# A two-layer decoder: the wide heads' output product in f16 parts, and one PSUM ring for two kinds of sums

## The reference, cut to what matters

```python
q = (x @ w_q);  k = (cond @ w_k);  v = (cond @ w_v)       # 16 heads of 64
a = softmax(q @ k.T / sqrt(64))                            # 112 x 375 to a head
x = layernorm(x + (a @ v).reshape(b, 112, 1024) @ w_out + b_out)
```

## Time and profile before

| | |
|---|---|
| median of three runs | 1141.89 us (1140.78 to 1142.65) |
| the profiled execution | 1142.11 us, of which the span of its instructions is 1140.3 us |
| TensorE, matmul | 977.3 us busy, 86% of the span |
| TensorE, weight loads | 703.0 us, 62%, beside the matmuls |
| VectorE | 661.8 us, 58% |
| ScalarE | 589.5 us, 52% |
| GpSimd | 285.3 us, 25% |
| granted clock of TensorE, mean | 0.924 of full speed |
| the chain that ended last | TensorE 52%, VectorE 22%, ScalarE 10%, DMA 5% |

### The profile page before, as it was taken

One profiled execution on the slowest core, in us unless ns is written; L12 is line 12 of the kernel. 1 busy time (PEld: TensorE's weight loads), 2 busy tenths in 40 slices (PEclk: granted clock), 3 DMA queues, 4 the chain that ended last, 5 costly groups with the idle time before them and its releaser, 6 DMA issues.

```text
span 1140.3 us, 22115 instructions
## 1 busy us (share of the span) xinstructions
PE 977.3 (86%) x8864; PEld 703.0 (62%) x8864; DVE 661.8 (58%) x1565; ACT 589.5 (52%) x1379; POOL 285.3 (25%) x297
## 2 busy tenths in 40 slices
PE   7987889897879898999898688888889897699995
PEld 4664556665469775567566556666666665447654
DVE  3256545665848855665666477676676664436103
ACT  5532555552548865555544355545555554465741
POOL 3421422100420007121112122122222205132733
PEclk9997878988989999999999899999899798689998
DMA  9351554300769868532261433221221105000001
GB/s 304 108 95 34 122 107 83 96 12 20 245 201 346 292 234 257 178 107 89 78 199 59 116 109 109 82 74 63 83 84 53 28 1 231 1 1 1 1 1 33
DMA packets 66678, 123.71 MB, mean 108 GB/s; under 512 B 11632, under 2 KB 41968, under 8 KB 62496
## 3 DMA queue, kind: packets, MB, share of 16 engines
q1 hardware_dynamic: 64528, 117.48, 33.8%
q0 software_dynamic: 2048, 4.82, 1.4%
HBM read 86.30 MB, written 35.92 MB: 107 GB/s over the span
## 4 chain that ended last, share of the span: by engine, by line
PE 52%; DVE 22%; ACT 10%; DMA 5%; POOL 4%; issue 4%; SPq 1%; DVEq 0%; POOLq 0%; ACTq 0%
PE psum L405 36%; ACT s_p L2738 3%; DVE s_p L2780 3%; DVE s_max L2769 2%; PE psum L1402 2%; PE psum L2708 2%; PE psum L2697 2%; DMA raw_wd<-in_wd 2%; DVE s_pT L2761 1%; POOL got L2003 1%; PE psum L2227 1%; DMA ctx_raw<-in_ctxT 1%; PE psum L560 1%; PE psum L2876 1%; DVE s_max L679 1%
## 5 line engine op out<-in xcount | busy, mean ns | idle before, releaser
L2738 ACT ACTIVATE s_p<-psum,s_max 112x375 f32<-112x375 f32 x128 | 72.2, 569 | 97.6 <-DVE s_max L2769 97.6
L726 POOL TENSOR_TENSOR rstd<-meanvar,minus_half 112x1 f32<-112x1 f32 x40 | 25.1, 629 | 244.7 <-DVE meanvar L671 174.2
L679 DVE TENSOR_REDUCE s_max<-psum 112x2 f32<-112x750 f32 x64 | 59.4, 934 | 35.7 <-PE psum L560 35.0
L2697 PE MATMUL psum<-ident,s_p 112*125 112x112 f32 x384 | 62.7, 296 | 8.9 <-DVE s_p L2780 4.2
L2769 DVE TENSOR_REDUCE s_max<-psum 112x1 f32<-112x375 f32 x128 | 63.7, 539 | 1.9 <-PE psum L2689 1.9
L2697 PEld LDWEIGHTS psum<-ident,s_p 112*125 112x125 f32 x384 | 51.3, 198 | 19.0 <-DVE s_p L2780 6.1
L3079 POOL TENSOR_TENSOR rs<-ms,minus_half 112x32 f32<-112x32 f32 x8 | 43.5, 5440 | 77.5 <-DVE ms L3013 77.5
L2689 PE MATMUL psum<-s_k,s_q 64*112 64x375 f16 x384 | 46.5, 348 | 18.5 <-ACT s_p L2738 6.3
L405 PE MATMUL psum<-Wv,ctx 128*125 128x512 f16 x240 | 58.6, 394 | 3.5 <-issue 2.7
L405 PE MATMUL psum<-ctx,Wk 128*128 128x375 f16 x320 | 61.5, 327 | 0.0
L3397 POOL TENSOR_TENSOR hidden<-raw,hidden 128x448 f16<-128x448 f32 x44 | 45.5, 1036 | 54.8 <-ACT hidden L3280 53.0
(11 more groups left out here) (381 smaller groups left out, 2465.1 us busy)
## 6 DMA issues: line engine op xcount, KB each, us to landing
keys<-s_k SPq DMA_DIRECT2D x64, 187.5 KB, 2.3
s_k<-keys SPq DMA_DIRECT2D x8, 1500.0 KB, 7.6
values<-s_v SPq DMA_DIRECT2D x48, 224.0 KB
s_v<-values SPq DMA_DIRECT2D x16, 672.0 KB
raw_wg<-in_wg SPq DMA_DIRECT2D x8, 1024.0 KB, 6.7
raw_wu<-in_wu SPq DMA_DIRECT2D x8, 1024.0 KB, 7.0
raw_wd<-in_wd SPq DMA_DIRECT2D x8, 1024.0 KB
s_kd<-k_halves SPq DMA_DIRECT2D x48, 93.8 KB, 3.8
```

What stands on the lines that cost most here:

```text
L679: VE.tensor_reduce(s1_max[b % 2][:, 2 * p:2 * p + 2], rings["s1"][unit][0:N, :, 0:S], X, ALU.max, negate=True).then_inc(*V.up("max1", n))
L2697: ins = TE.transpose(rings["t4"][unit][0:SCH, c * N:(c + 1) * N], p[:, c * SCH:(c + 1) * SCH], ident[0:N, 0:N])
L2738: SC.activation(rings["p4"][2 * n + j], rings["s4"][(n, j)][0:N, 0:S], ACT.Exp, bias=s4_max[b % 2][:, h:h + 1], accum_out=s4_sum[b % 2][:, ...
```

## The change

The output weights of the wide heads are split into f16 parts in stage 3, by ScalarE and VectorE, in a second `w4s` unit placed when the fourth `out` is placed. The raw weights now lie behind the raw query weights; the parts need the memory that the raw weights had. ScalarE's copy `oT4` writes f16, and a new unit `oT4l` has VectorE make the low part from the same bank, behind ScalarE. `s4_heads` places it one turn after `oT4`, ahead of the next group's sums; it, and no longer `oT4`, releases the bank, and `s4_out` waits for it. The output product is 24 f16 products in place of 8 f32 ones, and the add is the scaled one. The banks 6 and 7 become one ring for the wide and the causal sums.

```diff
-    Wq4 = g_w4.load(Region(nc, wts.base + keys_at, 20 * KB), "Wq4", [P, KC, HW])
-    Wq4_16 = ringm.tensor("Wq4_16", [P, 2, KC, HW], F16)
-    Wo4 = g_w4.load(ringm, "Wo4", [P, HW // P, D])
+    raw_w4 = Region(nc, wts.base + keys_at, 20 * KB)
+    w4_raw = {"Wq4": g_w4.load(raw_w4, "Wq4", [P, KC, HW]),
+              "Wo4": g_w4.load(raw_w4, "Wo4", [P, HW // P, D])}
+    w4_16 = {"Wq4": ringm.tensor("Wq4_16", [P, 2, KC, HW], F16),
+             "Wo4": ringm.tensor("Wo4_16", [P, 2, HW // P, D], F16)}
     bout4 = g_w4.load(ringm, "bout4", [N, D])
-    s4_attT = ringm.tensor("s4_attT", [P, HW // P, N])
+    s4_attT = ringm.tensor("s4_attT", [P, 2, HW // P, N], F16)
...
     def s3_ahead():
         yield from until(("out", 3, 2))
-        yield [("w4s",)]
+        yield [("w4s", "Wq4")]
+        yield from until(("out", 3, 3))
+        yield [("w4s", "Wo4")]
         yield from until(("k4put", 0, HP - 1), ("out", 3, 3))
...
             elif what == "w4s":
+                name, = at
                 act.wait_ge(g_w4.ready, V["got", 2, B - 1])
-                SC.activation(Wq4_16[:, 0], Wq4[:], ACT.Copy, scale=WSCALE).then_inc(*A.up("w4s"))
+                SC.activation(w4_16[name][:, 0], w4_raw[name][:], ACT.Copy,
+                              scale=WSCALE).then_inc(*A.up("w4s", name))
...
             elif what == "w4s":
-                dve.wait_ge(A["w4s",])
-                VE.scalar_tensor_tensor(Wq4_16[:, 1], Wq4[:], WSCALE, Wq4_16[:, 0], ALU.mult,
-                                        ALU.subtract).then_inc(*V.up("w4s"))
+                name, = at
+                dve.wait_ge(A["w4s", name])
+                VE.scalar_tensor_tensor(w4_16[name][:, 1], w4_raw[name][:], WSCALE, w4_16[name][:, 0],
+                                        ALU.mult, ALU.subtract).then_inc(*V.up("w4s", name))
...
-    w4 = banks(0, 6, by_release=True)
-    rings.update(s4=w4, t4=w4, misc4=w4, misc5=w4, o4=banks(6, 1), o5=banks(7, 1),
+    w4, sums = banks(0, 6, by_release=True), banks(6, 2, by_release=True)
+    rings.update(s4=w4, t4=w4, misc4=w4, misc5=w4, o4=sums, o5=sums,
                  p4=Ring(s4_p), pT4=Ring(s4_pT), sc5=Ring(sc5), pT5=Ring(pT5))
...
     step("oT4", "A oT4")
+    step("oT4l", "V oT4")
...
                 yield [("sc4", n)]
+            if o > 0 and o % 4 == 0:
+                place(("oT4l", (o - 1) // HP, (o - 1) % HP // 4))
             if 0 <= o < B * HP:
                 if o % 4 == 0:
                     yield from until(("vget", o // 4))
-                    rings["o4"].take(o // 4, (A, ("oT4", o // HP, o % HP // 4)))
+                    rings["o4"].take(("o4", o // 4), (V, ("oT4", o // HP, o % HP // 4)))
                 yield [("av4", o)]
...
     def s4_out(b):
-        yield from until(("oT4", b, 1))
+        yield from until(("oT4l", b, 1))
...
-                    rings["o5"].take(at[0], (A, ("oT5", at[0])))
+                    rings["o5"].take(("o5", at[0]), (A, ("oT5", at[0])))
...
             elif what == "out":
                 s, b = at
-                pe.wait_ge(A["oT4", b, 1], *rings["misc4"].free(unit))
+                pe.wait_ge(V["oT4", b, 1], V["w4s", "Wo4"], *rings["misc4"].free(unit))
                 mm(rings["misc4"][unit][0:N, 0:D],
-                   [(s4_attT[:, k, :], Wo4[:, k, :]) for k in range(HW // P)], T.up("out", 4, b))
+                   [(s4_attT[:, u, k, :], w4_16["Wo4"][:, v, k, :])
+                    for k in range(HW // P) for u, v in PARTS], T.up("out", 4, b))
...
-                SC.activation(s4_attT[:, 4 * q:4 * q + 4, :],
-                              rings["o4"][2 * b + q][:, 0:4 * N].rearrange("p (t n) -> p t n", n=N),
+                SC.activation(s4_attT[:, 0, 4 * q:4 * q + 4, :],
+                              rings["o4"]["o4", 2 * b + q][:, 0:4 * N].rearrange("p (t n) -> p t n", n=N),
                               ACT.Copy).then_inc(*A.up("oT4", b, q))
...
             elif what == "out":
                 s, b = at
-                vector_add(4, b, 0, res, G["bias", 4, b], rings["misc4"][unit][0:N, 0:D])
+                vector_add_scaled(4, b, res, G["bias", 4, b], rings["misc4"][unit][0:N, 0:D])
+            elif what == "oT4l":
+                b, q = at
+                dve.wait_ge(A["oT4", b, q])
+                VE.scalar_tensor_tensor(
+                    s4_attT[:, 1, 4 * q:4 * q + 4, :],
+                    rings["o4"]["o4", 2 * b + q][:, 0:4 * N].rearrange("p (t n) -> p t n", n=N), 1.0,
+                    s4_attT[:, 0, 4 * q:4 * q + 4, :], ALU.mult,
+                    ALU.subtract).then_inc(*V.up("oT4", b, q))
```

More of the change, by code:

```diff
@@ L580, in tensor_ends @@
             ring = rings[f"misc{s}"]
-            pe.wait_ge(x_ch_at(3, b), x_ch_at(3, b + 1), V["w4s",], *ring.free(unit))
+            pe.wait_ge(x_ch_at(3, b), x_ch_at(3, b + 1), V["w4s", "Wq4"], *ring.free(unit))
             mm(ring[unit][:, 0:2 * N],
-               [(Wq4_16[:, u, k, t * P:(t + 1) * P], x16[:, v, k, b * N:(b + 2) * N])
+               [(w4_16["Wq4"][:, u, k, t * P:(t + 1) * P], x16[:, v, k, b * N:(b + 2) * N])
                 for k in range(KC) for u, v in PARTS], T.up("q4", s, b, t))
@@ L2704, in tensor_s4 @@
                 if p % 4 == 0:
-                    pe.wait_ge(*rings["o4"].free(n // 4))
+                    pe.wait_ge(*rings["o4"].free(("o4", n // 4)))
                 for c in range(NCH):
                     for j in range(2):
-                        ins = TE.matmul(rings["o4"][n // 4][64 * j:64 * j + 64, p % 4 * N:(p % 4 + 1) * N],
+                        ins = TE.matmul(rings["o4"]["o4", n // 4][64 * j:64 * j + 64, p % 4 * N:(p % 4 + 1) * N],
                                         s4_v[n // 4 % 3][:, c, 2 * (p % 4) + j, :],
@@ L2887, in tensor_s5 @@
         elif what == "av5":
-            q, o = at[1], rings["o5"][b]
+            q, o = at[1], rings["o5"]["o5", b]
             if q == 0:
-                pe.wait_ge(*rings["o5"].free(b))
+                pe.wait_ge(*rings["o5"].free(("o5", b)))
             pe.wait_ge(V["pT5", b, 2 * q + 1], A["v5", b])
@@ L2971, in scalar_s5 @@
             act.wait_ge(T["av5", b, 1])
-            SC.activation(oT5[b % 2][:], rings["o5"][b][:, 0:4 * N].rearrange("p (g n) -> p g n", n=N),
+            SC.activation(oT5[b % 2][:], rings["o5"]["o5", b][:, 0:4 * N].rearrange("p (g n) -> p g n", n=N),
                           ACT.Copy).then_inc(*A.up("oT5", b))
```

## The result

The changed kernel takes 1157.34 us (median of four runs, 1152.6 to 1162.49) where the kernel before took 1142.27 us (median of four runs beside them, 1140.78 to 1145.77): a ratio of 1.0105, 95% interval 1.0062 to 1.0149. That is 15 us slower, and outside the predicted range of 1131.5 to 1147.

The account below looks back on a forecast made before the run. No engine was taken as full: a ring of dependent steps bounds the wide stage, TensorE busiest (87%). Terms -8.2 + 3.4 + 3.5 - 3 + 1.1 = -3.2 us gave 1138.7 us, range 1131.5 to 1147.

Parts of the forecast that it names:

- the ring: Wide and causal sums sharing two banks: old waits saved, new waits at four group boundaries; +3.5 us in all.
- the place of the product: Wide output products issued later, behind the next scores, so VectorE's residual adds idle less: -3 us, bounds 0 and -5.6.
- the split: Splitting the output weights in the causal stage makes TensorE wait for VectorE: +1.1 us, bounds 0 and 3.1.
- the low part: Sixteen new VectorE units of 0.615 us in the wide stage, partly covered by slack: +3.4 us, bounds 0 and 9.8.
- the products: Eight wide output products on TensorE's chain take 2.62 us in f16 instead of 3.64 in f32: -8.2 us.
- The rule of the Trainium skill that was weighed: Judge TensorE by busy weight loads: products would cost +2.3 us, total +7.3, 1149.2 us; as a rival, 2%.
- +5, bounds 0 and 7.3: New waits of sums for VectorE's low part at four boundaries with causal sums live, partly found again: +5 us.
- The old waits: TensorE's three waits for ScalarE's copy at new groups, 3.0 us, go; half counted, -1.5 us.
- TensorE held at the ring, slower: Rival: the four boundary waits cost all 7.3 us and the lower clock 3.4 more; +5.5, 1147.4 us; 22%.
- The whole gain: Rival: low part hidden but for the last pair, boundary waits found again, old ones gone; -10.6, 1131.3 us; 18%.
- VectorE decides: Rival: all 9.8 us of the low part's units on VectorE are paid; about 0, 1142 us; 13%.
- All three signs of being wrong: Sums waiting over four times or 8 us; lower-clock stretch growing over 3 us; a product over 3 us.

Follow-up runs that it names:

- e4: Changed kernel without the low part's unit: the product takes the high part in its place, ScalarE's copy releases the bank; 1141.01 us, ratio 0.998.
- e5: Changed kernel with the low part's unit reading the high part in SBUF, ScalarE's copy releasing the bank; 1139.51 us, ratio 0.9982.
- e7: Changed kernel with three banks for the sums and five for the rest, in place of two and six; 1148.73 us, ratio 1.0069.
- e1: Changed kernel with one bank each for wide and causal sums in place of the shared two; 1196.53 us, ratio 1.0475.
- e12: Changed kernel with the low part's unit cut to 16 columns from 448, the product taking the high part instead; 1154.21 us, ratio 1.0074.
- e2: Kernel before with only the two sums' banks made one ring, f32 product and ScalarE's release kept; 1142.0 us, ratio 0.9986.
- e8: Kernel before with seven of the eight wide output products issued one turn later, still f32; 1140.86 us, ratio 0.9985.
- e6: Changed kernel with the low part's unit placed ahead of the next head's maxima on VectorE; 1143.17 us, ratio 1.0006.
- e3: Changed kernel without the split of the output weights, the product reading the query weights' parts instead; 1155.7 us, ratio 1.0119.
- e10: Changed kernel with the low part ahead of the next maxima and the weight split in four pieces of 512 columns; 1148.37 us, ratio 1.0024.

## Why the prediction was wrong, step by step

In the stretches the change is made up so: products -9.5 (e4 against before), the low part's unit with the place of the product +6.3 (e5 against e4), the late release +12.9 (change against e5), together +9.7 from the first wide scores on; the split +3.8 (136.0 against 132.2, in e4 to e7), and +1.8 for the lower clock around the last two causal products. Both traces of the change have these 1.8 us, but e1, e4 to e7 and e12 don't, with the same program up to there, so they are not shown to be a price of the change. The sum is 15.3 of the 15.4; terms under some 2 us rest on single traces and are uncertain.

The forecast was -3.2, so 18.5 us have to be explained: the ring missed by 9.4 of them, the place of the product by 3.9, the split by 2.7, the low part by 2.0, the clock in the causal stage is 1.8, and the products were 1.3 better than said.

- **The products, -8.2: about right.** The record says 2.76 us at the upper clock against the 2.62 that I took from the causal stage, which would be 8 x 0.88 = 7.0 us; e4 puts the whole at -9.5. The rule of the Trainium skill that was weighed (Perfetto Trace Analysis, "Identifying the Most-Contended Engine") is meant for judging the engine's headroom. Taken as a forecast of what two forms of a product cost, as I took it, it fails here: from the first wide scores to the last copy of the causal sums the weight loads were busy for 219.2 us before and 218.7 in e4, and the stretch went from 349.9 to 340.8 us.
- **The ring, +3.5: this is the step that failed.** I took "+5, bounds 0 and 7.3" for four waits. There were five, 13.0 us, and two of them were *causal* sums taking a bank that the low part had just left, a case that I had not counted. Of the wide sums' three, two were 2.43 us, as the 2.4 worked out for the first kind of boundary; the third was 3.04. I had priced VectorE's queue from the trace of before, as it stands at two boundaries, but not the case that an instruction ahead of the unit waits for GpSimd (2.25 us of the 3.87 at 885). Two errors in the idle time cancel, which is luck: the waits are 13.0 us and not 7.3, but more than half of them is found again elsewhere (e5), and the idle time of TensorE grows by 5.6 us, close to the +5. What the step put at nothing is the slower work behind the waits, which stood only in the rival: 7.3 us. Together, by e5, the late release costs 12.9 us.
- **The old waits, -1.5: wrong, small.** e2: they go and nothing is gained.
- **The low part, +3.4: under its cost, within its bounds.** Its length was right (616 ns). e4 to e5 says +6.3 for the unit and the later product together; e8 puts the later product at +0.9 in f32. So some 5.4, inside 0 to 9.8. e12 against the change gives 2.2 us for 16 x 0.45 us; there the time is ruled by the ring anyway.
- **The place of the product, -3: wrong.** The adds' idle time fell as foreseen (e8: 23.0 to 14.6), but over both stretches nothing came of it: +0.9, and the ratio's interval (0.9954 to 1.0016) allows 5 us less to 2 more. I had counted half of an idle time of VectorE as time of the kernel, in a loop in which TensorE has the same work either way.
- **The split, +1.1, bounds 0 and 3.1: too low.** 3.7 us at its place, above the upper bound. The bound was the wait of the twin on TensorE (3.07); here the idle time is 1.9 us, and the rest is slower work behind it (1.8).

The rival *TensorE held at the ring, slower* named the mechanism and both of its prices, waits and clock. It had 22% and 1147.4 us; its point of decision (waits and clock together over 6 us) was passed by far. It still priced the clock too low (3.4 us). The range was also misread when it was set: 1147 lies below this rival's own 1147.4, so it can't hold "most of the ring's case". *The whole gain* and *VectorE decides* fall. All three signs of being wrong came: five waits with 13.0 us in all, products over 3 us (3.41 to 4.83 us for four of the eight), and more time at the lower clock. My estimate of the last from the mean clocks: from the first wide scores on some 81 us before (0.94 over 291.9 us, 0.89 over 209.1) and some 101 after (0.93 over 297.1, 0.86 over 213.6).

What stays open: why e7's runs are some 5 us slower than its trace lets one expect, where 2.5 of e4's 9.5 us come from, and what sets off the lower clock at the seventh causal product in one kernel and not in another with the same program. Putting the low part on GpSimd, or on VectorE from an f32 copy in SBUF with the bank released by ScalarE, was not tried; e5 bounds it at about the time of before as long as VectorE has the unit.

## What to carry to other kernels

When a change gives a buffer a second reader on another engine, the price is not the reader's 0.6 us but its place in that engine's queue: list what stands ahead of it at every reuse of the buffer, including instructions that wait for a third engine, and try the unit right behind its input (e6: 9.2 of the 12.9 us back with one moved line). Price an idle piece of TensorE together with the slower work behind it; here it was more than the idle time again. And idle time that a view shows before an instruction (the residual add's 23.0 us) is not a gain until something that sets the end waits for that instruction.

## What the hardware showed that I had not expected

The same instructions behind the same wait run at either clock: the seventh causal output product took 2.83, 4.22, 4.49 and 5.37 us in before, e3, e10 and the change, each time behind 2.59 us of idle TensorE. Even the same program, with the same time from the first causal output product to the seventh within 0.3 us, does so: 5.37 us in the change, 2.83 in e1, e4 to e7 and e12. So a wait on its own does not decide the clock here, and a trace of one kernel can hold 2 us that belong to no edit. The mean clock of the wide scores' stretch followed the idle time: 0.96, 0.93 and 0.85 with 43, 49 and 65 us idle (e5, the change, e1), and the busy time of the same records (2338, 2338, 2337) rose from 240 to 248 and 272 us. The Trainium skill (TensorE: Matmul & The Clock Gate, "What's actually happening") ties the clock to the engine's recent activity, and these three rows agree. And the two traces of the changed kernel repeat to 0.1 us in all stretches behind the first 500 us, while that first part, the same code in all kernels, varied by 22 us.
